# Free matmuls in the pauses of the last stage, its maxima by columns and its blocks half by half, and a third key diagonal in the rotary attention

## The chip, the cores and the metric

One NeuronCore of one Trainium2 chip. The time is the device time of one launch, in microseconds (us). PE is TensorE (PEld its weight loads), DVE VectorE, ACT ScalarE, POOL GpSimd, SP the engine that issues most DMAs.

## The reference, cut to what matters

Two layers over x (16 x 64 tokens of 512 numbers): cross attention over a context, self attention, MLP; each is added to x. The change touches the last two of these six parts.

```
# rotary self attention: 16 heads of 64, 16 sequences of 64 tokens
q, k = rope(xn @ Wq + bq), rope(xn @ Wk + bk);  v = xn @ Wv + bv
x = x + softmax(causal(q @ k.T / 8)) @ v @ Wo + bo
# quantized MLP, I = 1408
fake_quant(t, clip): scale = sigmoid(clip) * max(|t|) / 127
                     return clip(round(t / scale), -128, 127) * scale
xq = fake_quant(layernorm(x), clip_x)                 # max over ALL of x
h  = fake_quant(silu(xq @ wg.T) * (xq @ wu.T), clip_down)  # max over ALL of h
x  = x + h @ wd.T                                     # weights rounded per row
```

Both maxima run over the whole tensor, so nothing can be rounded before the last row of it is there.

## The kernel before

The 1024 tokens are 8 tiles of 128 rows, in `xres`.

**Rotary attention** (`rotary_attention`, L1495) takes two tiles at a time: four turns, the first and the last written out, the two between in a loop. The engines' orders are written by hand, with semaphores. In a turn PE projects four groups of keys and four of queries (n = 0 to 7; group 0 of the keys is done in the turn before), three products of high and low halves each, into `PROJ_BANK`, each group in 24 matmuls. ACT adds the bias (L1743, into `pair`), DVE multiplies by cosine and sine (L1885, two instructions into `s_e`), POOL adds (L1962, L1963) into `kT` or `qT`; `pair` and the products have one buffer, so this chain takes one group after another. The scores of a group (L1624) are one product per pair of heads against a block diagonal of its keys, `k_diag`, that DVE makes from `kT` (`spread_keys`, L1870, two instructions). There are two such buffers for eight groups in a turn (two tiles s, four groups g): group 4s+g waits until the scores of the group two before it are done (L1868). Groups 0 and 1 are spread ahead of the products of n = 4 and 5, all others behind n = 7. Then come the maxima (L1830), exponentials (L1767), transposes, products with the values (`attend`, L1645, which waits for the copies of the values, L1824) and the output projection (L1669), `x` (L1854) and its statistics.

**Last stage** (`FfnFront`, L1395, and `quantized_ffn`, L2294). Each tile is normalised on DVE (L1489), its largest absolute value taken (L1492), transposed on PE (L1461) and copied by ACT (L1466). Tile 7 is last. Then the maximum over columns (L2432), spread over partitions by a transpose (L2369), the step and its inverse (L2438 to L2442). ACT multiplies and rounds `xT` in eight pieces, four per half of the tokens (L2417), DVE clips (L2449, L2451) and makes the steps (L2454). PE multiplies blocks of 128 of the 1408 columns by halves of 512 tokens: gate and up, four matmuls each (L2379 for the first two blocks, L2362 for 20 more), with one pair of banks per half, so a block waits for the multiplication of the block two before it. ACT takes silu (L2423) after gate and up, DVE multiplies (L2459) and takes maxima (L2464), two blocks at a time but one by one for the last two. The second maximum, step and inverse follow; then ACT rounds `inner` tile by tile (L2427; tile 0 in three pieces of 3, 4 and 4 chunks), DVE clips (L2496, L2498), PE multiplies by the down weights, 11 matmuls a tile (L2397), the last tile in two halves (L2405), and DVE scales (L2481). Two of the eight results are added on the core, six by accumulating DMAs of POOL.

Of the kernel before, what the change touches and what calls it, by code (L numbers as in the profile page):

```python
# [17 lines left out]
P = 128  # L18
# [38 lines left out]
class Front:  # L57
# [12 lines left out]
    @staticmethod  # L70
    def reserve(sb, name):

        sb(name, [P, 24 + 2 * D + 4 * KC * P])

# [1196 lines left out]
class RotaryFront:  # L1271


    def __init__(self, core, tag, heads, io, scale):
# [17 lines left out]
        with ExitStack() as early:  # L1292
# [5 lines left out]
            Front.reserve(sb, "over_front")  # L1298
# [96 lines left out]
class FfnFront:  # L1395
# [36 lines left out]
    def open_semaphores(self):  # L1432
# [9 lines left out]
        self.rowmax_ok = sem("rowmax_ok")  # L1442
        self.xT_done = sem("xT_done")
# [9 lines left out]

    def transpose(self, pe, t):
        pe.wait_ge(self.xn_ok, t + 1)
# [37 lines left out]


def rotary_attention(core, block, rot, front, x_done, scale, ffn, finished):  # L1495
# [9 lines left out]
    AHEAD = TURNS  # L1505
    with ExitStack() as st:
# [14 lines left out]
        PROJ_BANK = [6, 7, 0, 1]  # L1521
# [51 lines left out]
        def _(pe):  # L1573
# [34 lines left out]
            def open_scores():  # L1608

                for s in range(2):  # L1610
                    for n in range(NB):
                        pe.matmul(bank[S_BANK[s][n]][:, :], ident_b[:, :], mask_sb[:, :, :].rearrange("p a b -> p (a b)"),
                                  start=True, stop=False, skip_group_check=True)

            def scores(i, s, groups):
                for g in groups:
# [4 lines left out]
                    for a in range(AB):  # L1621
                        for b in range(2):
                            tokens = slice(s * P + b * SEQ, s * P + (b + 1) * SEQ)
                            mm = pe.matmul(at[SEQ * b:SEQ * (b + 1), cols], qT[:, g, a, tokens], k_diag[g % 2][:, a, b, :],  # L1624
                                           start=False, stop=(a == AB - 1), skip_group_check=True)
# [46 lines left out]
            def turn(i, first, last=False):  # L1672
# [50 lines left out]
            for t in range(4, TILES):  # L1723
                ffn.transpose(pe, t)

        @block.scalar
        def _(act):
# [59 lines left out]
            for t in range(2, TILES):  # L1787
                ffn.copy(act, t)

        @block.vector  # L1790
        def _(dve):
# [69 lines left out]
            def turn(i, first, last=False):  # L1861
# [3 lines left out]
                def spread_keys(s, g):  # L1865
                    if 4 * s + g >= 2:

                        dve.wait_ge(s_done, 8 * i + 4 * s + g - 1)  # L1868
                    for a in range(AB):
                        ins = dve.tensor_tensor(  # L1870
                            k_diag[g % 2][:, a, :, :].rearrange("p b (j n) -> p b j n", j=4),
# [4 lines left out]
                for n in range(2 * GROUPS):  # L1876
                    if n in (4, 5):
# [12 lines left out]
                spread_keys(0, 2)  # L1890
# [52 lines left out]
            ffn.normalise(dve, 2, TILES - 1)  # L1943
# [350 lines left out]
def quantized_ffn(core, block, ffn, out):  # L2294
# [6 lines left out]
    HD = D // 2  # L2301
    with ExitStack() as st:
# [20 lines left out]
        g_done = sem("g_done")  # L2323
        silu_ok = sem("silu_ok")
        h_ok = sem("h_ok")
        hmax_ok = sem("hmax_ok")
        hr_a = sem("hr_a")
        hr_b = sem("hr_b")
# [26 lines left out]
        def _(pe):  # L2355
            def gate_and_up(i):
                for s in range(HALVES):
                    if i:
                        pe.wait_ge(h_ok, 2 * (i - 1) + s + 1)
                    for w, bank in ((gT, g_bank), (uT, u_bank)):  # L2360
                        for k in range(KC):
                            mm = pe.matmul(bank[s][:, :], w[:, k, i * P:(i + 1) * P],  # L2362
                                           xT_q[:, k, s * HT:(s + 1) * HT], start=(k == 0), stop=(k == KC - 1))
                    mm.then_inc(g_done, 1)
# [6 lines left out]
            def first_gate_and_up():  # L2371

                pe.wait_ge(gate_in, 16)
                pe.wait_ge(up_in, 16)
                for s in range(HALVES):
                    for k in range(KC):
                        pe.wait_ge(xq_ok, KC * s + k + 1)
                        for w, bank in ((gT, g_bank), (uT, u_bank)):
# [292 lines left out]
```

## Time and profile before

| what | value |
|---|---|
| three runs | 1086.51, 1084.78, 1086.65 us; median 1086.51 |
| profiled execution | 1084.72 us, its span 1082.9 us |
| mean granted clock of PE | 0.995 |
| PE busy | 1053.9 us (97%), x6156 |
| DVE, ACT, POOL busy | 635.0, 347.2, 204.4 us |

A row of a timeline is: start, duration, engine, line, operation, output and inputs, count, and in brackets the idle time of the engine before it and what ended that. Instructions of one line are merged. The granted clock is 1.00 at 2.4 GHz and 0.50 at 1.2 GHz.

### The profile page before, as it was taken

How to read it: one execution, taken by the hardware profiler on the slowest of the kernel's cores; microseconds unless marked ns; L12 is line 12 of the kernel's file. 1: busy time of each engine (PE TensorE's matmuls, PEld its weight loads, DVE VectorE, ACT ScalarE, POOL GpSimd, SP SyncE). 2: the span in 40 equal slices, each digit the busy share in tenths (PEclk: the TensorE clock that was granted, in tenths of full speed). 3: DMA queues.
4: the chain of work that ended last, by engine and by line, in shares of the span. 5: the costliest groups of instructions: out<-in, count | busy, mean ns of one | idle time of the engine just before them, and what ended most of it. 6: DMA issues, size and time to landing. Idle time of an engine off the chain costs nothing.

```text
span 1082.9 us, 16786 instructions
## 1 busy us (share of the span) xinstructions
PE 1053.9 (97%) x6156; PEld 660.2 (61%) x6172; DVE 635.0 (59%) x1116; ACT 347.2 (32%) x984; POOL 204.4 (19%) x201
## 2 busy tenths in 40 slices
PE   9999999999999999999999999999999999999887
PEld 5556658888544444444444466657788696877333
DVE  3344346877856621357652275557866758468677
ACT  2422256566521110220001032236332524226434
POOL 0011101333222230000002511131214133040002
PEclk9999999999999999999999999999999999999998
DMA  9996802001026680025547469963000000040105
GB/s 349 378 335 220 331 1 79 2 0 40 20 95 205 118 38 1 0 84 165 168 120 266 159 210 365 367 238 117 2 1 1 2 1 0 0 156 16 59 1 77
DMA packets 68609, 129.59 MB, mean 120 GB/s; under 512 B 9424, under 2 KB 13520, under 8 KB 68176
## 3 DMA queue, kind: packets, MB, share of 16 engines
q1 hardware_dynamic: 67696, 127.38, 36.3%
q0 software_dynamic: 864, 1.57, 1.2%
q8 instruction: 29, 0.48, 0.2%
q14 instruction: 20, 0.16, 0.0%
HBM read 120.92 MB, written 8.01 MB: 119 GB/s over the span
## 4 chain that ended last, share of the span: by engine, by line
PE 66%; issue 11%; DVE 10%; POOL 5%; ACT 3%; SPq 2%; DMA 1%; DVEq 0%; POOLq 0%; ACTq 0%
PE bank L2126 26%; PE bank L2153 5%; PE bank L474 5%; PE bank L442 4%; PE bank L396 3%; PE bank L2362 3%; PE bank L972 2%; PE bank L1669 2%; PE bank L519 2%; PE bank L508 2%; DVE s_e L1885 2%; PE bank L2397 2%; ACT s_e L1063 2%; PE bank L494 2%; DMA x_proj<-in_x_pw_dram 1%
## 5 line engine op out<-in xcount | busy, mean ns | idle before, releaser
L2171 ACT ACTIVATE f_act<-bank,f_sgn 128x512 f32<-128x512 f32 x64 | 44.0, 687 | 261.8 <-PE bank L2126 257.3
L2126 PE MATMUL bank<-f_a_lo,f_w 128*128 128x512 f16 x512 | 115.7, 379 | 0.0
L2126 PE MATMUL bank<-f_a_hi,f_w 128*128 128x512 f16 x512 | 115.7, 379 | 0.0
L2126 PEld LDWEIGHTS bank<-f_a_lo,f_w 128*128 x512 | 50.1, 98 | 60.4
L2126 PEld LDWEIGHTS bank<-f_a_hi,f_w 128*128 x512 | 50.1, 98 | 60.2
L2226 DVE CAST f_b_hi<-f_act 128x512 f16<-128x512 f32 x32 | 26.6, 833 | 96.9 <-ACT f_act L2171 96.8
L1885 DVE TENSOR_TENSOR s_e<-s_pair,s_tables 128x512 f32<-128x512 f32 x64 | 41.4, 688 | 37.2 <-POOL s_kT L1963 21.6
L442 PE MATMUL bank<-x_cT,x_qT 128*64 128x512 f32 x256 | 58.5, 598 | 0.0
L474 PE MATMUL bank<-x_cN,x_eT 128*64 128x512 f32 x256 | 56.9, 596 | 0.0
L1767 ACT ACTIVATE s_e<-bank,s_nmax 128x64 f32<-128x64 f32 x128 | 38.1, 337 | 31.5 <-DVE s_nmax L1830 31.3
L2282 POOL TENSOR_SCALAR f_w<-f_upper_bits 128x2048 bf16<-128x2048 uint8 x16 | 31.3, 1957 | 76.1 <-PE bank L2126 76.1
L1870 DVE TENSOR_TENSOR s_k_diag<-s_kT,s_spread 128x512 f32<-128x512 f32 x64 | 44.6, 754 | 1.1 <-PE bank L1624 1.0
L738 DVE TENSOR_TENSOR x_aT_lo<-bank,x_aT_hi 128x512 fp32r<-128x512 f32 x16 | 11.1, 691 | 56.6 <-ACT x_aT_hi L599 56.5
L1063 ACT ACTIVATE s_e<-bank,s_nmax 128x64 f32<-128x64 f32 x128 | 38.1, 350 | 7.0 <-DVE s_nmax L1134 6.9
L773 POOL TENSOR_TENSOR x_mv<-x_mv,eps 128x2 f32<-128x2 f32 x10 | 1.9, 192 | 200.5 <-DVE x_mv L631 200.5
L474 PEld LDWEIGHTS bank<-x_cN,x_eT 128*64 128x64 f32 x256 | 17.6, 137 | 32.8 <-issue 32.6
L1624 PE MATMUL bank<-s_k_diag,s_qT 128*64 128x256 f32 x256 | 32.9, 389 | 3.6 <-DVE s_k_diag L1870 2.1
L442 PEld LDWEIGHTS bank<-x_cT,x_qT 128*64 128x64 f32 x256 | 16.9, 136 | 31.2 <-issue 30.8
L1962 POOL TENSOR_TENSOR s_kT<-s_e 128x256 f32<-128x256 f32 x16 | 13.3, 832 | 111.7 <-DVE s_e L1885 111.7
L780 POOL MEMSET x_ones<- 128x128 f32 x1 | 0.2, 204 | 179.3 <-DMA x_bk<-in_x_kb_dram 179.3
L2262 DVE SCALAR_TENSOR_TENSOR xres<-bank,f_out_scale,xres 128x512 f32<-128x512 f32 x8 | 6.0, 751 | 47.0 <-PE bank L2153 47.0
L2126 PE MATMUL bank<-f_xT_hi,f_w 128*128 128x512 f16 x128 | 32.9, 379 | 0.0
(341 smaller groups left out, 2309.4 us busy)
## 6 DMA issues: line engine op xcount, KB each, us to landing
x_cT<-in_ctx_cols_dram SPq DMA_DIRECT2D x32, 1024.0 KB, 9.0
x_cN<-in_ctx_rows_dram SPq DMA_DIRECT2D x32, 1024.0 KB, 11.6
f_upper_bits<-in_f_w_dram SPq DMA_DIRECT2D x20, 256.0 KB, 4.1
f_row<-in_f_wg_dram SPq DMA_DIRECT2D x11, 256.0 KB, 3.2
f_long_row<-in_f_wd_dram SPq DMA_DIRECT2D x4, 704.0 KB, 6.4
f_row<-in_f_wu_dram SPq DMA_DIRECT2D x11, 256.0 KB, 3.1
f_part<-in_f_wgT_dram SPq DMA_DIRECT2D x8, 352.0 KB, 3.5
f_part<-in_f_wuT_dram SPq DMA_DIRECT2D x8, 352.0 KB, 3.2
```

The source lines that it names most:

```text
L396: mm = pe.matmul(bank[Q_BANK[half]][:, a * PT:(a + 1) * PT], l[:, k, c * P:(c + 1) * P], r[:, k, :], start=(m == 0 and k == 0), stop=(m == ...
L442: mm = pe.matmul(bank[S_BANK[s]][SEQ * b:SEQ * (b + 1), :], qT[:, k, tokens], cT[s][:, b, k, :], start=(k == 0), stop=(k == KC - 1))
L474: mm = pe.matmul(bank[AV_BANK[s]][SEQ * b:SEQ * (b + 1), :], eT[s][:, k, SEQ * b:SEQ * (b + 1)], cN[s][:, b, k, :], start=(k == 0), stop=( ...
L1063: ins = act.activation(e_sb[s][n][:, j * SEQ:(j + 1) * SEQ], bank[S_BANK[s][n]][:, j * SEQ:(j + 1) * SEQ], ACT.Exp, bias=nmax[s][:, h:h + ...
L1624: mm = pe.matmul(at[SEQ * b:SEQ * (b + 1), cols], qT[:, g, a, tokens], k_diag[g % 2][:, a, b, :], start=False, stop=(a == AB - 1), skip_gr ...
L1767: ins = act.activation(e_sb[n][:, j * SEQ:(j + 1) * SEQ], bank[S_BANK[s][n]][:, j * SEQ:(j + 1) * SEQ], ACT.Exp, bias=nmax[s][:, h:h + 1], ...
L1870: ins = dve.tensor_tensor(k_diag[g % 2][:, a, :, :].rearrange("p b (j n) -> p b j n", j=4), kT[:, g, a, s * P:(s + 1) * P].rearrange("p (b ...
L1885: ins = dve.tensor_tensor(flat(prods[t]), flat(pair[:, :, :]), table(t), ALU.mult)
L2126: mm = pe.matmul(h_bank[s][:, :], weights(2 * i + s, k), part[:, k, cols], start=(n == 0 and k == 0), stop=(n == 1 and k == k_chunks - 1))
L2153: mm = pe.matmul(y_bank[t % 2][:, :], part[:, k, t * P:(t + 1) * P], w2_sb[:, k, :], start=(n == 0 and k == 0), stop=(n == 1 and k == HC - 1))
L2171: act.activation(act32[s][:, :], h_bank[s][:, :], ACT.Relu, scale=sgn[:, layer % 2:layer % 2 + 1]).then_inc(h_read, 1)
L2362: mm = pe.matmul(bank[s][:, :], w[:, k, i * P:(i + 1) * P], xT_q[:, k, s * HT:(s + 1) * HT], start=(k == 0), stop=(k == KC - 1))
```

## The change

In the last stage of `rotary_attention` and in `quantized_ffn`:

- `keep_busy` issues matmuls whose result nobody reads: 8 behind the transposes of tiles 4 to 6, 6 behind that of tile 7, 7 behind the last block and 9 behind the second spread of the maxima.
- Tile 7 is centred first (no root needed), its maximum taken and that column multiplied by the root; ACT scales the rows beside it. The spread of the maxima now stands ahead of tile 7's transposes, and ACT rounds the first half of `xT` before it copies tile 7.
- The first four blocks go (0,0), (1,0), (0,1), (1,1) (column block, half); banks and silu buffers go by block number. Gate and up have a semaphore each, so silu starts after the gate.
- DVE multiplies and rounds the first piece of `inner` itself; ACT starts with the second.

In the rotary attention a third `k_diag` lies in the place of the normalised rows; keys of group 2 are spread ahead of n = 6; groups 2 and 3 are projected into banks 2 and 3; the masks of the first tile and its first scores no longer wait for the last read of the queries.

```diff
+        slots.append(sb("k_diag2", shape))
+    def keep_busy(self, pe, count, free):
+        for _ in range(count):
+            pe.matmul(self.core.bank[free][:, :], self.gT[:, 0, 0:P], self.gT[:, 0, 0:D], start=True, stop=True)
+    def centre_last(self, dve):
+        t = TILES - 1
+        dve.wait_ge(self.xT_done, t - 5)
+        dve.tensor_scalar(self.xn[t % 6][:, :], self.core.xres[:, t, :], self.mv[:, t, 0:1], None, ALU.subtract).then_inc(self.centred, 1)
+        dve.wait_ge(self.centred, 1)
+        dve.tensor_reduce(self.a_rows[:, t:t + 1], self.xn[t % 6][:, :], AX_X, ALU.max, apply_absolute_value=True).then_inc(self.centred, 1)
+        dve.wait_ge(self.centred, 2)
+        dve.wait_ge(self.rstd_ok, 3)
+        dve.tensor_tensor(self.a_rows[:, t:t + 1], self.a_rows[:, t:t + 1], self.rstd[:, t:t + 1], ALU.mult).then_inc(self.rowmax_ok, 1)
+    def scale_last(self, act):
+        act.wait_ge(self.centred, 2)
+        act.wait_ge(self.rstd_ok, 3)
+        act.activation(self.xn[t % 6][:, :], self.xn[t % 6][:, :], ACT.Copy, scale=self.rstd[:, t:t + 1]).then_inc(self.last_ok, 1)
...
-        PROJ_BANK = [6, 7, 0, 1]
+        PROJ_BANK = [6, 7, 2, 3]
-                    if n == 2:
-                        pe.wait_ge(x_ok, 2 * i + 1)
...
                 pe.wait_ge(k_read, GROUPS * (i + 1))
+                pe.wait_ge(x_ok, 2 * i + 1)
+                open_scores(0)
+                scores(i, 0, (0, 1))
                 pe.wait_ge(q_read, GROUPS * (i + 1))
-                open_scores()
-                scores(i, 0, (0, 1))
+                open_scores(1)
                 project_values(0, (1,))
...
-            for t in range(4, TILES):
+            for t in range(4, TILES - 1):
                 ffn.transpose(pe, t)
+            pe.wait_ge(ffn.gate_in, 16)
+            ffn.keep_busy(pe, 8, 5)
...
-                    if 4 * s + g >= 2:
-                        dve.wait_ge(s_done, 8 * i + 4 * s + g - 1)
+                    n = 4 * s + g
+                    if n >= KD:
+                        dve.wait_ge(s_done, 8 * i + n - KD + 1)
-                    if n in (4, 5):
+                    if n in (4, 5, 6):
                         spread_keys(0, n - 4)
                 copy_values(i, 0, (0,))
-                spread_keys(0, 2)
                 spread_keys(0, 3)
...
+    BLOCKS = [(0, 0), (1, 0), (0, 1), (1, 1)] + [(i, s) for i in range(2, IC) for s in range(HALVES)]
...
             spread_maxima(0)
-            first_gate_and_up()
-            for i in range(1, IC):
-                gate_and_up(i)
+            ffn.transpose(pe, TILES - 1)
+            pe.wait_ge(up_in, 16)
+            ffn.keep_busy(pe, 6, 5)
+            for n in range(len(BLOCKS)):
+                if n in (0, 2):
+                    gate_and_up_by_chunk(n)
+                else:
+                    gate_and_up(n)
+            pe.wait_ge(h_ok, len(BLOCKS) - 1)
+            ffn.keep_busy(pe, 7, 4)
             spread_maxima(1)
+            ffn.keep_busy(pe, 9, 4)
...
-            act.wait_ge(xT_ok, TILES)
+            act.wait_ge(xT_ok, TILES // 2)
             for s in range(HALVES):
+                if s == 1:
+                    ffn.copy(act, TILES - 1)
+                    act.wait_ge(xT_ok, TILES)
...
+                if n == 0:
+                    dve.tensor_scalar(part, part, a_inv[:, 1:2], ROUND, ALU.mult, ALU.add).then_inc(first_ok, 1)
+                    dve.wait_ge(first_ok, 1)
+                else:
+                    dve.wait_ge(hr_a, n)
```

## Rows read from the trace of the kernel before

**Rows 1.** The page: its span, and PE's granted clock in 40 slices (tenths)

```profile
span 1082.9 us, 16786 instructions
...
PEclk9999999999999999999999999999999999999998
```

**Rows 2.** Timeline of DVE in the third turn of the rotary attention

```profile
890.17 1.29 DVE L1885 TENSOR_TENSOR s_e<-s_pair,s_tables 128x512 f32<-128x512 f32 x2 [0.63 <-POOL s_kT L1963]
891.38 1.84 DVE L1870 TENSOR_TENSOR s_k_diag<-s_kT,s_spread 128x512 f32<-128x512 f32 x2
893.84 1.29 DVE L1885 TENSOR_TENSOR s_e<-s_pair,s_tables 128x512 f32<-128x512 f32 x2 [0.63 <-POOL s_qT L1963]
896.68 1.29 DVE L1885 TENSOR_TENSOR s_e<-s_pair,s_tables 128x512 f32<-128x512 f32 x2 [1.54 <-POOL s_qT L1963]
...
904.99 0.69 DVE L1830 TENSOR_REDUCE s_nmax<-bank 128x8 f32<-128x512 f32 x1
905.96 2.50 DVE L1870 TENSOR_TENSOR s_k_diag<-s_kT,s_spread 128x512 f32<-128x512 f32 x4 [0.28 <-PE bank L1624]
```

**Rows 3.** Timeline of POOL in the same turn

```profile
891.54 1.13 POOL L1962 TENSOR_TENSOR s_qT<-s_e 128x256 f32<-128x256 f32 x1 [1.41 <-DVE s_e L1885]
892.62 1.19 POOL L1963 TENSOR_TENSOR s_qT<-s_e 128x256 f32<-128x256 f32 x1
895.22 0.73 POOL L1962 TENSOR_TENSOR s_qT<-s_e 128x256 f32<-128x256 f32 x1 [1.41 <-DVE s_e L1885]
```

**Rows 4.** Timeline of PE in the same turn: the products with the values

```profile
913.21 1.97 PE L1645 MATMUL bank<-s_v_diag,s_pT 128*64 128x128 f32 x32
```

**Rows 5.** Timeline of DVE in the first turn and in the last

```profile
774.41 0.69 DVE L1830 TENSOR_REDUCE s_nmax<-bank 128x8 f32<-128x512 f32 x1
775.59 2.50 DVE L1870 TENSOR_TENSOR s_k_diag<-s_kT,s_spread 128x512 f32<-128x512 f32 x4 [0.49 <-PE bank L1624]
...
971.10 0.69 DVE L1830 TENSOR_REDUCE s_nmax<-bank 128x8 f32<-128x512 f32 x1
971.71 2.50 DVE L1870 TENSOR_TENSOR s_k_diag<-s_kT,s_spread 128x512 f32<-128x512 f32 x4
```

**Rows 6.** Timeline of all engines from tile 7 to the last block

```profile
1007.42 0.55 DVE L1489 TENSOR_SCALAR f_xn<-xres,f_mv,f_rstd 128x512 f32<-128x512 f32 x1 [0.67 <-POOL f_rstd L1482]
1008.71 0.59 ACT L1466 COPY f_xT<-bank 128x512 f32<-128x512 f32 x1 [1.79 <-PE bank L1461]
1010.14 5.75 ACT L2417 ACTIVATE f_xT<-f_xT,f_plus_round,f_a_inv 128x512 f32<-128x512 f32 x8 [0.84 <-DVE f_a_inv L2442]
1016.70 0.74 DVE L2459 SCALAR_TENSOR_TENSOR f_inner<-bank,f_step,f_silu 128x512 f32<-128x512 f32 x1
1017.50 1.04 PE L2362 MATMUL bank<-f_xT_q,f_gT 128*128 128x512 bf16 x4
...
1050.86 1.03 PE L2362 MATMUL bank<-f_xT_q,f_gT 128*128 128x512 bf16 x4
```

**Rows 7.** PE by quarter microseconds: length, busy time (count), granted clock, DMA share, GB/s

```profile
1056.25:1056.50 0.25, 0.00 (x0) 0.72 0.00 0
...
1063.00:1063.25 0.25, 0.25 (x2) 0.63 0.00 0
```

**Rows 8.** Timeline of all engines from the last silu to the second tile's product

```profile
1052.79 0.69 ACT L2423 ACTIVATE f_silu<-bank,f_step 128x512 f32<-128x512 f32 x1 [1.04 <-PE bank L2362]
1055.02 0.18 DVE L2476 TENSOR_REDUCE f_a_max<-f_h_max 128x1 f32<-128x22 f32 x1
1058.14 0.58 PE L2397 MATMUL bank<-f_dT,f_inner_q 128*128 128x512 bf16 x1 [2.57 <-DVE f_inner_q L2498]
1061.00 0.56 DVE L2498 TENSOR_SCALAR f_inner_q<-f_inner_q 128x1408 bf16<-128x1408 bf16 x1
1062.79 1.44 PE L2397 MATMUL bank<-f_dT,f_inner_q 128*128 128x512 bf16 x5
```

**Rows 9.** Groups of ACT by shape: ACT's first piece of `inner`

```profile
L2427 ACT ACTIVATE f_inner<-f_inner,f_plus_round,f_a_inv 128x384 f32<-128x384 f32 x1 | 0.7, 707 | 2.9 <-DVE f_a_inv L2442 2.9
```

More of the change, by code:

```diff
@@ L1505, in rotary_attention @@
     AHEAD = TURNS
+    KD = len(rot.k_diag)
     with ExitStack() as st:
@@ L1606, in project_values, with open_scores @@
                     mm.then_inc(v_done, 1)
[L1608 to L1613, printed above, removed]
+            def open_scores(s):
+                for n in range(NB):
+                    pe.matmul(bank[S_BANK[s][n]][:, :], ident_b[:, :], mask_sb[:, :, :].rearrange("p a b -> p (a b)"),
+                              start=True, stop=False, skip_group_check=True)
             def scores(i, s, groups):
@@ L1786, in _ @@
             act.preload_act_table(ACT.Silu)
-            for t in range(2, TILES):
+            for t in range(2, TILES - 1):
                 ffn.copy(act, t)
+            ffn.scale_last(act)
         @block.vector
@@ L2355, in _, with gate_and_up, gate_and_up_by_chunk @@
         def _(pe):
[L2356 to L2364, printed above, removed]
+            def gate_and_up(n):
+                i, s = BLOCKS[n]
+                if n >= 2:
+                    pe.wait_ge(h_ok, n - 1)
+                for w, bank, done in ((gT, g_bank, g_done), (uT, u_bank, u_done)):
+                    for k in range(KC):
+                        mm = pe.matmul(bank[n % 2][:, :], w[:, k, i * P:(i + 1) * P],
+                                       xT_q[:, k, s * HT:(s + 1) * HT], start=(k == 0), stop=(k == KC - 1))
+                    mm.then_inc(done, 1)
+            def gate_and_up_by_chunk(n):
+                i, s = BLOCKS[n]
+                if n >= 2:
+                    pe.wait_ge(h_ok, n - 1)
+                for k in range(KC):
+                    pe.wait_ge(xq_ok, KC * s + k + 1)
+                    for w, bank, done in ((gT, g_bank, g_done), (uT, u_bank, u_done)):
+                        mm = pe.matmul(bank[n % 2][:, :], w[:, k, i * P:(i + 1) * P], xT_q[:, k, s * HT:(s + 1) * HT],
+                                       start=(k == 0), stop=(k == KC - 1))
+                        if k == KC - 1:
+                            mm.then_inc(done, 1)
             def spread_maxima(n):
@@ L2418, in _ @@
             act.wait_ge(steps_ok, 2)
-            for i in range(IC):
-                for s in range(HALVES):
-                    act.wait_ge(g_done, 2 * i + s + 1)
-                    act.activation(silu[s][:, :], g_bank[s][:, :], ACT.Silu, scale=steps[0][:, i:i + 1]).then_inc(silu_ok, 1)
+            for n, (i, s) in enumerate(BLOCKS):
+                act.wait_ge(g_done, n + 1)
+                if n >= 2:
+                    act.wait_ge(h_ok, n - 1)
+                act.activation(silu[n % 2][:, :], g_bank[n % 2][:, :], ACT.Silu, scale=steps[0][:, i:i + 1]).then_inc(silu_ok, 1)
             act.wait_ge(astep_ok, 4)
-            for t, chunks in PIECES:
+            for t, chunks in PIECES[1:]:
                 part = inner[:, chunks, t * P:(t + 1) * P]
```

63 lines of the change are left out of this document (34 added, 29 removed).

## The prediction

> **What bounds the kernel now.** The page first: PE is granted its full clock in every slice but the last [rows 1], so the change has to be read from the timelines of two stretches, the rotary attention (four turns) and the last stage. In the rotary attention the timeline of DVE is what ends last between the last rope of a turn and the products with the values: DVE runs copy, spreads, maxima and spreads with one short wait, and PE's products with the values start when DVE's copies are there [rows 2, 4]. In the last stage four things follow each other that PE can't shorten: the maximum of x, the rounding of x, the maximum of h, the rounding of h. Rows 6 and 8 are that chain. Its last part is run at half clock: the granted clock leaves 1.00 inside 1056.25:1056.50, after a stretch in which PE had done one transpose since 1052.8, and is back inside 1063.00:1063.25 [rows 7]. It fell once before, about 1012, inside the first chain.
>
> **Rotary attention.** A rope group comes every 2.84 us (893.84 to 896.68), and every 3.67 us where a spread stands ahead of it (890.17 to 893.84): 0.83 us more, because POOL's two additions take 1.13 and 1.19 us beside the spread and 0.73 alone [rows 2, 3]. A third spread at n = 6 thus delays the last rope of a turn by 0.83 us. In return one spread of four halves, half of 2.50, so 1.25 us, goes from DVE's run behind the last rope [rows 2]. And the spread of the second tile's group 0 waits for a diagonal: from maximum to spread it takes 0.97 us in the third turn (904.99 to 905.96), 1.18 in the first (774.41 to 775.59), and 0.61 in the last, where nothing is waited for [rows 2, 5]. With three diagonals it needs the scores of the group three before it, which PE has then done. So a turn gains 1.25 - 0.83 = 0.42, plus 0.57, 0.36, 0.36 and 0 us of that wait: 0.99 + 0.78 + 0.78 + 0.42 = 2.97 us. I take 2.9. What is late next is PE itself: it would finish its second transposes some 0.3 us ahead of the copies, so up to 0.8 us a turn fits, barely. PE's own earlier masks and scores are worth nothing on top, since DVE decides when `attend` starts; they cover that the last read of the queries also comes 0.83 us later. The wait that is added (x_ok ahead of the first masks) has project_outputs and add of the turn before behind it, some 20 us ago. The banks only change who waits, at nothing: the banks 2 and 3 were read long before. Bounds: the spread's cost is between nothing (POOL's time alone) and 1.25 us (all of it), the gain of a turn between 0 (another engine takes over at once) and 1.25 + 0.57; for four turns 0 to 5 us, and if the delay came back nowhere, a loss of 4 x 0.83 = 3.3.
>
> The Trainium skill bears on the third spread. Its page "SBUF — State Buffer", section "Who interferes with whom", says that a VectorE instruction with two SBUF inputs contends with a GpSimd one that reads SBUF, and that the second to issue is blocked until the first has ended. Taken strictly, one addition would wait for most of one spread half and the next for all of another, about 1.2 us a turn for 0.83, and the four turns would gain 1.5 us for 2.9. The rows have 0.83, so I keep that.
>
> **The first chain.** Centring doesn't wait for the root: the 0.67 us in which DVE waited for POOL go [rows 6]; one multiplication of a column is added, about 0.2 us (the column reduction at 1055.02 takes 0.18 [rows 8]). The inverse is there 0.45 us earlier. But ACT's eight pieces (5.75 us, 0.71 apart) now have the copy of tile 7 in their middle, 0.59 us alone, some 0.62 with its wait [rows 6]; before, that copy lay in ACT's idle time. ACT's last piece ends 0.15 us later than before, and DVE multiplies only after it has clipped all eight pieces. So the first multiplication stays at about 1016.75 and the third block of PE at 1017.55 against 1017.50 [rows 6]: +0.05 us. Blocks (0,0) and (1,0) are both done by about 1015.6 and PE stands idle for 2 us; nothing comes of the new order. Bounds: if the copy were free, -0.45; if the scaling on ACT (a piece of 0.8 us, finished about when the inverse is there) pushed the pieces back by all of it, +0.8.
> The free matmuls here cost nothing: at 0.22 us each (four in 1.04 with the last one's own time [rows 6]) the 8 end at about 1007.8, ahead of the spread at 1008.5, and the 6 at about 1011.0, ahead of the first clipped piece at 1011.4. That half clock near 1012 slowed only matmuls that waited for DVE anyway.
>
> **The blocks.** From the third block (1017.50) to the last (1050.86) are 19 blocks in 33.36 us, 1.756 each; eight matmuls at 0.216 make 1.73 [rows 6]. The difference is the wait for the multiplication of two blocks before. With silu behind the gate alone it ends 0.87 us earlier, so the wait is met: -0.5 us. The same at the end: the last product ends at 1052.76, silu, multiplication and maximum follow, and the reduction starts at 1055.02, 2.26 us later [rows 8]. With silu already done, the multiplication starts at once, and DVE is free by then; 0.69 + 0.03 us of silu go: -0.7 us. Bounds: 0, where DVE is the one that is late, to -0.87.
>
> **The second chain and the down product.** The first product starts at 1058.14 and has its 11 matmuls in 4.65 us (0.42 each, the half clock), so the second tile starts at 1062.79 [rows 8]. Its input had been ready since 1061.56 (1061.00 + 0.56). At full clock tile 0 takes 2.4 us and the second tile would start at 1061.6; the two matmuls at half clock behind 1062.79 cost 0.3 more: the clock is worth 1.5 us. With ACT's first piece (0.707 us, 0.62 to the next [rows 9]) done by DVE instead, ACT reaches tile 1 0.62 us earlier, and the second tile, which waits for that and not for PE, starts 0.62 us earlier again. That the first product starts 0.4 us earlier is worth nothing. After that PE runs 2.375 us a tile as now. Together -2.1 us. Does the clock hold? Between the last block and the down product PE would have 7 free matmuls (1.5 us), 0.4 us idle, a transpose, 9 more (1.9 us) and 0.3 us idle, against one transpose in 5.4 us. The 9 end before the first product could start. Bounds for this part: 0 (the clock falls all the same and ACT's piece is lost in it) to -2.6.
>
> **The sum** for the profiled execution: -2.9 + 0.05 - 0.5 - 0.7 - 2.1 = -6.2 us (rounded), 1084.72 to 1078.5. That execution was as fast as the fastest of the three runs (1084.78), 1.8 us under their median of 1086.51. From the median the same sum gives 1080.3. Part of the spread can be the clock's fall, which the change takes away; I can't tell how much, and put the median in the middle, at 1079.4.
>
> **The rivals.**
> Clock lost in the second pause. A free matmul may not count, or not enough: the clock falls at about 1056 as now and stays low for 6.8 us [rows 7]. Then the 9 free matmuls take 3.8 us for 1.9 and hold the first product back by 1.65, and tile 0 runs slow: second tile 2.7 us later than planned, 1078.5 + 2.7 = 1081.2, by the median 1082.1. For it: transposes around 1009 didn't prevent the fall. Against it: real matmuls of this shape brought the clock back both times.
> Rotary gain not there. The rope chain is 0.83 us late, and what DVE saves is taken by PE or ACT (exponentials, transposes) as the next bound: 0 instead of -2.9, 1082.3 by the median. For it: PE would be only 0.3 us ahead.
> On the other side: the rope chain becomes what ends last in each turn. If something else than DVE's run held `attend` back, the 0.83 us would be paid in all four turns (+3.3 instead of -2.9) and the result is 1079.4 + 6.2 = 1085.6, level; it is slower only if in addition to being late each spread costs POOL its full 1.25: +5.0 instead of -2.9, 1087.3. It decides from a delay of 0.83 + 0.2 us per turn with no return. Against it: the last turn shows DVE's run without any wait, from the last rope to the copies.
> The change doesn't do what it says: the free matmuls are there and the clock is full, but DVE, at 0.95 + 0.56 + 0.75 us a tile against 2.375, sets the down product's pace after the early start: 1.5 us of the 2.1 lost, 1080.9.
>
> **How the numbers follow.** Forecast 0.62, with its own range 1077.5 to 1081; clock lost 0.14; rotary gain missing 0.12; DVE's pace 0.07; the other side 0.05. The range reaches to the first two rivals and leaves out the other side: 1077.2 to 1083.0. A measurement of this kernel can tell 0.2%, 2.2 us, from no change. Faster by more: 0.93; within: 0.04 (the other side's level half and mishaps of two rivals at once); slower: 0.03.
>
> **What would show it.** The trace after: rope groups 3.67 us apart three times a turn; no wait of DVE for L1624's banks; `attend` 0.4 to 1 us earlier relative to the turn's start, turns of 64.5 us for 65.3. In the last stage: ACT's copy of tile 7 between its fourth and fifth piece, the third block 0.0 to 0.2 us from where it was relative to tile 7's statistics, blocks 1.73 us apart, 1.5 us from the last product to the second reduction, clock at 1.00 from there to the end, and the second tile's product waiting about 0.85 us for DVE with PE idle. The prediction is wrong if the clock is 0.50 anywhere behind 1050, if the turns stay at 65.3 us, or if the third block comes over 0.5 us earlier or later.

## The result, and the profile after

| | before | after |
|---|---|---|
| median | 1086.58 us (1084.78 to 1088.05, 4 runs) | 1079.36 us (1078.92 to 1079.75, 4 runs) |
| profiled execution | 1084.72 us, span 1082.9 | 1079.72 us, span 1077.8 |
| mean granted clock | 0.995 | 1.000 |

The ratio is 0.9937, 95% interval [0.9924, 0.9951]: faster by 0.6%, 6.8 us by the ratio. The forecast was 1079.4. The page after, span and granted clock by slices [rows 1]:

```profile
span 1077.8 us, 16886 instructions
...
PEclk9999999999999999999999999999999999999999
```

Cut at events that both kernels have, the two traces give the table (us; "sum of row t" is the start of DVE's addition of tile t to x; the block times are PE's). The first sum of x stands ahead of the four turns.

| stretch | before | after | difference | predicted |
|---|---|---|---|---|
| start to the sum ahead of the turns (nothing changed) | 745.85 | 747.00 | +1.15 | 0 |
| the four turns, to the sum of row 7 | 259.07 | 255.89 | -3.18 | -2.9 |
| to the third block | 12.58 | 12.47 | -0.11 | +0.05 |
| 19 blocks, to the start of the last | 33.36 | 32.82 | -0.54 | -0.5 |
| to the second reduction | 4.16 | 3.44 | -0.72 | -0.7 |
| to the second inverse | 1.19 | 1.18 | -0.01 | 0 |
| to the halves of the last tile | 21.02 | 19.07 | -1.95 | -2.1 |
| to the end of the span | 5.67 | 5.93 | +0.26 | 0 |
| outside the span | 1.82 | 1.92 | +0.10 | 0 |

The changed stretches give -6.51, the others +1.51, together the -5.00 between the two profiled executions. The +1.15 is not the change's: over the fourteen kernels profiled here, with the same work up to that point, the sum starts between 745.65 and 747.00, and this execution is the highest. Nor is the +0.26: that last stretch takes 5.64 to 6.22 us in the others.

**The rotary attention.** DVE in the third turn after, and the first two of PE's products with the values; the rows answer to [rows 2, 4]:

```profile
889.63 1.29 DVE L1924 TENSOR_TENSOR s_e<-s_pair,s_tables 128x512 f32<-128x512 f32 x2 [0.63 <-POOL s_kT L2001]
...
893.30 1.29 DVE L1924 TENSOR_TENSOR s_e<-s_pair,s_tables 128x512 f32<-128x512 f32 x2 [0.63 <-POOL s_qT L2001]
894.51 1.83 DVE L1909 TENSOR_TENSOR s_k_diag<-s_kT,s_spread 128x512 f32<-128x512 f32 x2
896.97 1.29 DVE L1924 TENSOR_TENSOR s_e<-s_pair,s_tables 128x512 f32<-128x512 f32 x2 [0.63 <-POOL s_qT L2001]
899.79 1.29 DVE L1924 TENSOR_TENSOR s_e<-s_pair,s_tables 128x512 f32<-128x512 f32 x2 [1.52 <-POOL s_qT L2001]
...
902.74 1.29 DVE L1909 TENSOR_TENSOR s_k_diag<-s_kT,s_spread 128x512 f32<-128x512 f32 x2
904.06 0.69 DVE L1868 TENSOR_REDUCE s_nmax<-bank 128x8 f32<-128x512 f32 x1
904.67 2.49 DVE L1909 TENSOR_TENSOR s_k_diag<-s_kT,s_spread 128x512 f32<-128x512 f32 x4
...
910.08 1.73 DVE L1862 TENSOR_TENSOR s_v_diag<-bank,s_bv_row 64x256 f32<-64x256 f32 x4
911.90 0.33 PE L1677 MATMUL bank<-s_v_diag,s_pT 128*64 128x128 f32 x2
```

A group with a spread ahead of it comes 3.67 us behind the one before (893.30 to 896.97), one without 2.82. Behind the last rope two spread halves are left for four, and the four behind the first maximum start 0.61 us after it and run without a wait, for 0.97 before [rows 2]. The products with the values start 36.25 us into the turn (from the sum of row 3, at 875.65) for 37.03 before (from 876.18) [rows 4]. The turns take 64.10, 64.55, 64.52 and 62.72 us, before 65.05, 65.28, 65.29 and 63.45: gains of 0.95, 0.73, 0.77 and 0.73.

**The first pause.** All engines after, which answers to [rows 6]:

```profile
1007.23 0.17 DVE L2496 RECIPROCAL f_a_inv<-f_a_step 128x1 f32<-128x1 f32 x1
1007.48 2.93 ACT L2471 ACTIVATE f_xT<-f_xT,f_plus_round,f_a_inv 128x512 f32<-128x512 f32 x4 [0.89 <-DVE f_a_inv L2496]
1010.31 0.56 ACT L1484 COPY f_xT<-bank 128x512 f32<-128x512 f32 x1
1010.91 2.93 ACT L2471 ACTIVATE f_xT<-f_xT,f_plus_round,f_a_inv 128x512 f32<-128x512 f32 x4
1014.56 1.41 DVE L2515 SCALAR_TENSOR_TENSOR f_inner<-bank,f_step,f_silu 128x512 f32<-128x512 f32 x2
1015.36 0.39 PE L2415 MATMUL bank<-f_xT_q,f_gT 128*128 128x512 bf16 x1 [1.78 <-DVE f_inner L2515]
```

ACT's copy of tile 7 stands between its fourth and fifth piece, and PE idles 1.78 us ahead of the third block.

**The second pause**, after, which answers to [rows 8]; L1467 are the free matmuls:

```profile
1049.24 0.69 ACT L2477 ACTIVATE f_silu<-bank,f_step 128x512 f32<-128x512 f32 x1 [1.04 <-DVE f_inner L2515]
...
1050.11 0.75 DVE L2515 SCALAR_TENSOR_TENSOR f_inner<-bank,f_step,f_silu 128x512 f32<-128x512 f32 x1
1050.89 0.69 DVE L2521 TENSOR_REDUCE f_h_max<-f_inner 128x1 f32<-128x512 f32 x1
1051.62 0.17 DVE L2533 TENSOR_REDUCE f_a_max<-f_h_max 128x1 f32<-128x22 f32 x1
...
1052.01 2.11 PE L1467 MATMUL bank<-f_gT 128*128 128x512 bf16 x9
...
1052.80 0.16 DVE L2496 RECIPROCAL f_a_inv<-f_a_step 128x1 f32<-128x1 f32 x1
...
1054.42 2.54 PE L2448 MATMUL bank<-f_dT,f_inner_q 128*128 128x512 bf16 x11 [0.30 <-DVE f_inner_q L2559]
...
1056.01 0.96 DVE L2557 TENSOR_SCALAR f_inner_q<-f_inner 128x1408 bf16<-128x1408 f32 x1 [0.42 <-ACT f_inner L2481]
...
1057.61 4.71 PE L2448 MATMUL bank<-f_dT,f_inner_q 128*128 128x512 bf16 x21 [0.66 <-DVE f_inner_q L2559]
```

Silu of the last block runs beside its second product. Tile 0 of the down product takes 2.54 us to the end of its last matmul; before it was 4.65 from its start to that of tile 1 [rows 8]. Then PE stands idle until DVE has clipped tile 1, and DVE had itself waited 0.42 for ACT.

### The profile page after: what moved, and what is told of

It reads as the page before. It is cut to its first block, busy times and chain, and to the rows that moved or that the text cites. A ratio compares the mean times of both kernels' runs of the same rounds, so it can differ in the third digit from the quotient of the medians.

```text
span 1077.8 us, 16886 instructions
## 1 busy us (share of the span) xinstructions
PE 1056.4 (98%) x6186; PEld 663.5 (62%) x6202; DVE 638.7 (59%) x1118; ACT 347.2 (32%) x984; POOL 207.9 (19%) x201
## 4 chain that ended last, share of the span: by engine, by line
PE 65%; issue 11%; DVE 10%; POOL 6%; ACT 3%; SPq 3%; DMA 1%; DVEq 0%; POOLq 0%; ACTq 0%
PE bank L2164 26%; PE bank L2191 5%; PE bank L482 5%; PE bank L450 4%; PE bank L404 3%; PE bank L2403 3%; PE bank L980 2%; PE bank L1701 2%; PE bank L527 2%; PE bank L516 2%; DVE s_e L1924 2%; ACT s_e L1071 2%; PE bank L502 2%; DMA x_proj<-in_x_pw_dram 1%; PE bank L2448 1%
## 5 line engine op out<-in xcount | busy, mean ns | idle before, releaser
L1909 DVE TENSOR_TENSOR s_k_diag<-s_kT,s_spread 128x512 f32<-128x512 f32 x64 | 47.1, 787 | 0.1
```

What stands on the lines that cost most here:

```text
L1909: ins = dve.tensor_tensor(k_diag[n % KD][:, a, :, :].rearrange("p b (j n) -> p b j n", j=4), kT[:, g, a, s * P:(s + 1) * P].rearrange("p ( ...
```

## The experiments

The twelve kernels were measured in three groups, each beside the kernel before, whose median moved between them (1085.81, 1085.37, 1085.94). So medians are compared within a group only, and across groups the ratios and the stretches of the traces, by the cuts of the table above.

### The rotary part alone

```
# the kernel before, with only the edits in rotary_attention and k_diag2
```

> The kernel before with the rotary edits alone; the last stage is untouched. Theory (DVE's run behind the last rope ends last in a turn, and a third diagonal shortens it): the four turns are 0.95, 0.73, 0.77 and 0.73 us shorter, as in the trace after, 3.2 us in all, and the time is 3.2 us under that of before. The last stage keeps both stretches at half clock, so the spread between runs stays as wide as that of before. Rival (the rotary edits move nothing of their own; the turns are shorter because of something in the last stage's code): turns of 65.3 us as before, no gain.

1082.60 us against 1085.81, ratio 0.9970 [0.9958, 0.9981], 3.2 us. Its four turns take 255.85 us, as in the changed kernel (255.89), 3.22 less than before. The rotary part adds up with the rest, and no engine outside DVE took the gain back. The clock still falls: 0.51 in 1053 to 1060. The seven runs lie within 1.3 us, the eleven of the kernel before beside them within 3.0, so the spread did not stay as wide as expected. The last stage is that of before, yet the stretch from the second inverse to the halves takes 20.80 us for 21.02: where the clock comes back moves it by 0.22 us between executions.

### No free matmuls, and those of the first pause alone left out

```diff
-        for _ in range(count):
+        for _ in range(0):
```

> The changed kernel without all 30 free matmuls; nothing else differs. Theory (only the second pause matters, because the first blocks wait for DVE): granted clock 0.50 again near the first blocks and from the second maximum into the down product. The down product's second tile starts 1.5 to 2 us later than in the changed kernel, the end comes 1.5 us later (0 to 3.4 us, by where the clock's fall and rise lie), and the third block starts where it did. Rival (the clock would hold anyway with the shorter pauses): clock 1.00, no difference. Rival (the first pause matters too): the third block or the blocks behind it are late, over 3 us in all.

```diff
-            ffn.keep_busy(pe, 8, 5)
...
-            ffn.keep_busy(pe, 6, 5)
```

> The changed kernel without the 8 and 6 free matmuls of the first two pauses; the 7 and 9 of the last two stay. Theory: the clock falls near the first blocks only, where PE waits for DVE, and costs 0 to 0.5 us; the down product starts and runs as in the changed kernel. Rival (a fall there is not over when the third block starts): the blocks behind 1015 run at half clock for up to 3 us, 1.5 us lost.

Without any: 1080.57 us (ratio 0.9953 [0.9939, 0.9967]); without the first 14: 1079.11 (0.9936 [0.9923, 0.9950]). Busy times by stretch without any free matmul (columns: length; PE, PEld, DVE, ACT, POOL busy with counts; granted clock; DMA share; GB/s):

```profile
1051.00:1053.00 2.00, 0.29 (x1) 0.13 (x1) 1.36 (x5) 0.78 (x2) 0.00 (x0) 0.63 0.00 0
1053.00:1058.00 5.00, 4.35 (x11) 1.64 (x12) 4.42 (x10) 5.00 (x5) 0.00 (x0) 0.50 0.00 0
```

and PE there, from the second block's last product to the third block:

```profile
1013.38 1.31 PE L2403 MATMUL bank<-f_xT_q,f_uT 128*128 128x512 bf16 x4
1014.54 0.38 PE L2415 MATMUL bank<-f_xT_q,f_gT 128*128 128x512 bf16 x1
```

Without those of the first pause:

```profile
1008.00:1010.00 2.00, 1.42 (x4) 0.66 (x6) 1.90 (x7) 1.97 (x4) 0.00 (x0) 0.50 0.98 369
1010.00:1013.00 3.00, 3.00 (x9) 1.04 (x8) 2.61 (x10) 3.00 (x5) 0.00 (x0) 0.50 0.75 279
...
1051.00:1053.00 2.00, 2.00 (x10) 0.70 (x8) 1.64 (x6) 1.09 (x2) 0.00 (x0) 1.00 0.00 0
```

From the inverse to the halves it is 20.53 us without any, and 19.08 with those of the second pause, as in the changed kernel (19.07): the clock is worth 1.46 us there. In the first pause the clock is 0.50 for 6.8 us in both kernels, and without the first 14 alone that costs nothing: from the sum of row 7 to the second reduction 48.73 us with them and 48.73 without, since PE waits there for DVE either way. Without any it takes 48.88. By the granted clock in half microseconds it came back some 0.8 us later behind the sum of row 7 in that execution (12.1 us for 11.2); PE had no idle time left ahead of the third block, as the rows show, and that block starts 12.64 us behind the sum for 12.47. So DVE hides the half clock with next to no margin: 0.00 us lost in one execution, 0.15 in the other. The stretch from the second reduction to the inverse is 0.07 longer without any as well (1.25 for 1.18); no cause of that is shown. All 30 free matmuls together are worth 1.68 us by these stretches.

### A third pair of banks

```diff
+    BLOCKS = [(0, 0), (1, 0), (2, 0), (0, 1), (1, 1), (2, 1)] + [(i, s) for i in range(3, IC) for s in range(HALVES)]
+    SETS = 3
-        core.bank[2:4], core.bank[4:6], core.bank[6:8]
+        core.bank[2:4], core.bank[4:6] + [core.bank[1]], core.bank[6:8] + [core.bank[2]]
-                if n >= 2:
-                    pe.wait_ge(h_ok, n - 1)
+                if n >= SETS:
+                    pe.wait_ge(h_ok, n - SETS + 1)
# the chunk-wise blocks are 0 and 3; free matmuls behind the last block go into bank 5
```

> The changed kernel with a third pair of banks (1 and 2, free by then) for gate and up: the first six blocks go (0,0), (1,0), (2,0), (0,1), (1,1), (2,1), a block waits for the multiplication of the block three before it, and the free matmuls of the last pauses go to bank 5. Theory (PE is idle for 1.8 us ahead of the third block only because both pairs of banks are taken, and DVE, with 1.33 us of work a block against PE's 1.73, catches up before the last block): the third block runs in that pause and all behind it come one block earlier, 1.7 us gained on the changed kernel. Rival (DVE's first multiplication at 1014.6 is the true start of the pipeline and its backlog reaches the end): 0 to 0.5 us gained.

1076.72 us (1076.32 to 1077.94), ratio 0.9918 [0.9904, 0.9931], 2.4 us under the kernel without the first free matmuls in the same group, of which 1.73 is the edit's by the traces; 0.57 lies in the last stretch (5.65 us for 6.22), which no edit touches. The stretch to the second reduction takes 47.00 us for 48.73, a whole block of 1.73 less. PE's idle time ahead of the third block is filled with one more block of the first half, and PE gets to the fourth (the first that needs the second half) only 0.2 us before DVE's multiplication frees its banks:

```profile
1013.26 1.41 DVE L2516 SCALAR_TENSOR_TENSOR f_inner<-bank,f_step,f_silu 128x512 f32<-128x512 f32 x2
1014.07 0.39 PE L2416 MATMUL bank<-f_xT_q,f_gT 128*128 128x512 bf16 x1
```

### ACT's first piece of h given back

```diff
-            for t, chunks in PIECES[1:]:
+            for t, chunks in PIECES:
...
-                if n == 0:
-                    dve.tensor_scalar(part, part, a_inv[:, 1:2], ROUND, ALU.mult, ALU.add).then_inc(first_ok, 1)
```

> The changed kernel, but ACT rounds the first piece of `inner` again and DVE only clips it. Theory: the second tile of the down product waits for ACT's fourth piece, so it starts one ACT piece (0.62 us from start to start) later and PE ends that much later; everything ahead of the second inverse as in the changed kernel: from the inverse to the last tile's halves 19.7 us for 19.07, time 1079.4 + 0.6 = 1080.0. Rival: DVE's clipping sets the pace of that stretch and not ACT: 0, 1079.4, and the wait ahead of the second tile as long as in the changed kernel.

1079.22 us, ratio 0.9944 [0.9931, 0.9958]. The time alone doesn't tell it from the changed kernel, the trace does: from the inverse to the halves 19.67 us for 19.07, +0.60. DVE waits for ACT ahead of tile 1, and PE behind it:

```profile
1055.44 0.96 DVE L2553 TENSOR_SCALAR f_inner_q<-f_inner 128x1408 bf16<-128x1408 f32 x1 [0.69 <-ACT f_inner L2481]
...
1057.05 5.14 PE L2448 MATMUL bank<-f_dT,f_inner_q 128*128 128x512 bf16 x23 [0.94 <-DVE f_inner_q L2555]
```

### Silu behind both products, with two waits and with one

```diff
-                act.wait_ge(g_done, n + 1)
+                act.wait_ge(u_done, n + 1)
```

> The changed kernel, but ACT's silu waits for the end of `up` and not of `gate`. Theory: the blocks are 1.756 us apart again for 1.727 (19 of them: +0.5 us) and the last product is followed by silu, multiplication and maximum in a row again (2.26 us to the second reduction for 1.55: +0.7), together +1.2, time 1080.6, and from the sum of row 7 to the second reduction 49.95 us for 48.73. Rival: the blocks were 1.727 apart because of the order of the blocks and silu buffers, not of the silu's start: only +0.7, 1080.1.

1080.50 us, ratio 0.9956 [0.9942, 0.9969]. From the sum of row 7 to the second reduction it takes 50.77 us, +2.04 and not +1.2. The blocks are 1.794 us apart, more than before the change (1.756). DVE here waits for the product and then for silu, and starts 0.10 us behind silu's end; before it was one wait and 0.03. So that was taken away:

```diff
-                dve.wait_ge(u_done, n + 1)
                 dve.wait_ge(silu_ok, n + 1)
```

> As the run with silu behind both products, but DVE's multiplication waits for silu alone and not for the product and silu. That run had the blocks 1.794 us apart and a multiplication 0.10 us behind silu's end, the kernel before 1.756 and 0.03. Theory: the second wait costs 0.07 us and stands in the loop that sets the pace there, so without it the blocks are 1.756 apart again, 0.7 us less in all: from the sum of row 7 to the second reduction 50.0 us for 50.77. Rival: the order of blocks or the silu buffers set it, and it stays at 50.7.

1079.75 us, ratio 0.9948 [0.9934, 0.9961]; 49.97 us to the second reduction, the blocks 1.756 apart. The last block with two waits:

```profile
1049.97 0.69 ACT L2477 ACTIVATE f_silu<-bank,f_step 128x512 f32<-128x512 f32 x1 [1.04 <-PE bank L2403]
1050.76 0.75 DVE L2515 SCALAR_TENSOR_TENSOR f_inner<-bank,f_step,f_silu 128x512 f32<-128x512 f32 x1 [0.25 <-ACT f_silu L2477]
```

and with one:

```profile
1049.52 0.69 ACT L2477 ACTIVATE f_silu<-bank,f_step 128x512 f32<-128x512 f32 x1 [1.04 <-PE bank L2403]
1050.24 0.75 DVE L2514 SCALAR_TENSOR_TENSOR f_inner<-bank,f_step,f_silu 128x512 f32<-128x512 f32 x1 [0.17 <-ACT f_silu L2477]
```

From the start of silu to that of the multiplication it is 0.79 us against 0.72. The early silu is worth 49.97 - 48.73 = 1.24 us, as the two terms of the prediction say. The second wait that the change adds costs 0.07 us a multiplication where it lies on the path (why an already satisfied wait costs that, no run shows), so 0.04 a block (1.794 for 1.756), since a block waits for the multiplication of the block two before, and 0.8 in all; in the changed kernel a multiplication ends some 0.7 us before its banks are needed, which hides it.

### Tile 7 as before, and tile 7 rounded straight from its bank

```diff
-            act.wait_ge(xT_ok, TILES // 2)
+            act.wait_ge(xT_ok, TILES)
...
-            ffn.centre_last(dve)
+            ffn.normalise(dve, 2, TILES - 1)
# transposes of tile 7 ahead of the spread, its copy ahead of ACT's rounding
```

> The changed kernel, but tile 7 is normalised, its maximum taken, transposed and copied ahead of the spread and of ACT's rounding, as before the change; the free matmuls, the order of the blocks and the semaphores stay. Theory: the inverse is 0.45 us later and ACT's last rounding piece at most 0.15 us from where it was, so the third block starts within 0.15 us of where it does (12.47 us behind the sum of row 7; 12.58 in the kernel before): time 1079.3 to 1079.5. Rival: the new order is worth what it takes from the inverse's path: +0.45, third block 12.9 us behind, 1079.85.

1079.02 us, ratio 0.9942 [0.9928, 0.9955]; the third block is 12.58 us behind the sum of row 7 for 12.47. The whole new order of tile 7 is worth 0.1 us. ACT's pieces start 0.63 us later relative to the sum of row 7 (5.22 us behind it for 4.59), but run without the copy in their middle and end level (10.97 us behind it for 10.95):

```profile
1007.52 5.75 ACT L2464 ACTIVATE f_xT<-f_xT,f_plus_round,f_a_inv 128x512 f32<-128x512 f32 x8 [0.84 <-DVE f_a_inv L2489]
...
1014.08 1.40 DVE L2508 SCALAR_TENSOR_TENSOR f_inner<-bank,f_step,f_silu 128x512 f32<-128x512 f32 x2
1014.88 0.39 PE L2412 MATMUL bank<-f_xT_q,f_gT 128*128 128x512 bf16 x1 [1.25 <-DVE f_inner L2508]
```

```diff
-                    ffn.copy(act, TILES - 1)
+                    act.activation(xT[:, :, (TILES - 1) * P:], ffn.bank[TILES - 1][:, :].rearrange("p (k n) -> p k n", k=KC),
+                                   ACT.Identity, bias=plus_round[:, 0:1], scale=a_inv[:, 0:1]).then_inc(xr_a, 1)
# and the four pieces of the second half only 384 wide
```

> The changed kernel, but ACT no longer copies tile 7: it multiplies and rounds it straight out of its bank in one instruction (128x512), and its four pieces of the second half shrink to 384 columns. Theory: from the inverse to the third block ACT is what ends last, so four pieces shorter by about 0.1 us each (0.62 from start to start for 0.72, as the 128x384 and 128x512 pieces of the second rounding show) bring the third block 0.4 us forward, from 12.47 to 12.07 us behind the sum of row 7: 1079.0. Rival: DVE's clipping (0.67 to 0.72 us a piece) is as late as ACT and takes the place: at most 0.1, 1079.3.

1079.44 us (1078.25 to 1081.00), ratio 0.9944 [0.9930, 0.9957]: the times tell nothing of 0.2 us. By the trace the third block is 12.28 us behind the sum of row 7, -0.2, half of what ACT saves (its last piece ends 10.58 us behind the sum for 10.95):

```profile
1010.10 2.49 ACT L2473 ACTIVATE f_xT<-f_xT,f_plus_round,f_a_inv 128x384 f32<-128x384 f32 x4
...
1010.82 0.43 DVE L2505 TENSOR_SCALAR f_xT_q<-f_xT 128x512 bf16<-128x512 f32 x1 [0.23 <-ACT f_xT L2473]
...
1011.49 0.42 DVE L2505 TENSOR_SCALAR f_xT_q<-f_xT 128x512 bf16<-128x512 f32 x1
```

DVE waits for the first of these pieces only and then clips one in 0.67 us without a pause: it has taken ACT's place. Neither theory is right by itself: in the changed kernel ACT ends last, but only 0.2 us behind what DVE's own pace would allow.

### Two diagonals, and the masks back in their place

```diff
-                    if n in (4, 5, 6):
+                    if n in (4, 5):
...
+                spread_keys(0, 2)
                 spread_keys(0, 3)
# and k_diag2 gone, so KD = 2
```

> The changed kernel with two key diagonals for three (keys of group 2 spread behind the last rope again), the banks of groups 2 and 3 and the place of the masks and first scores as changed. Theory: all of the rotary gain is DVE's, so it goes: from the sum of x that ends turn 0 to that of turn 3 as in the kernel before, some 0.75 us a turn longer, 3.2 us for four turns: 1082.6. Rival: PE's masks and scores ahead of the last read of the queries carry a part of it, in the wait for the diagonals (0.97, 0.97, 0.61 us from maximum to spread before): then turns of 64.9 and 1.2 to 1.6 us in all, 1080.6 to 1081.

1081.65 us, ratio 0.9963 [0.9950, 0.9977]. The turns take 258.61 us: 2.72 of the 3.18 us went, and 0.46 stay with PE's order, less than the rival said and more than the theory. The masks' place was then turned back with three diagonals:

```diff
                 pe.wait_ge(x_ok, 2 * i + 1)
-                open_scores(0)
-                scores(i, 0, (0, 1))
                 pe.wait_ge(q_read, GROUPS * (i + 1))
+                open_scores(0)
                 open_scores(1)
+                scores(i, 0, (0, 1))
```

> The changed kernel with three diagonals, but PE's masks and first scores wait for the last read of the queries again. The run with two diagonals lost 2.72 us over the turns of the 3.18 gained, so 0.46 is left for PE's order. Theory A: that 0.46 is a part of the wait for a diagonal, which three diagonals take away anyway: here nothing is lost, the turns from the sum of row 1 to that of row 7 take 255.9 us. Theory B: it is a gain of its own and adds up: 256.35 us.

1081.01 us, ratio 0.9955 [0.9941, 0.9968]; the turns take 257.26 us, 1.37 more than 255.89, about 0.34 in each. Both theories fall: nothing lost, and 256.35. DVE's third turn shows what ends last then:

```profile
903.87 0.69 DVE L1868 TENSOR_REDUCE s_nmax<-bank 128x8 f32<-128x512 f32 x1
904.48 1.28 DVE L1909 TENSOR_TENSOR s_k_diag<-s_kT,s_spread 128x512 f32<-128x512 f32 x2
906.05 1.29 DVE L1909 TENSOR_TENSOR s_k_diag<-s_kT,s_spread 128x512 f32<-128x512 f32 x2 [0.30 <-PE bank L1656]
```

The spread of the second tile's group 0 starts at once, as the third diagonal lets it; that of its group 1 needs the scores of group 2 and waits 0.30 us for them, as in the other three turns (0.28 to 0.29). The four corners, in us for the four turns:

| | masks late | masks early |
|---|---|---|
| two diagonals | 259.07 | 258.61 |
| three diagonals | 257.26 | 255.89 |

Alone the edits are worth 1.81 and 0.46, together 3.18: 0.91 us come only with both. The corner with two diagonals and masks late is the kernel before, which also has groups 2 and 3 in banks 0 and 1 and the wait for `x_ok` there; no run has these alone, so their share of 1.81 and 0.46 is not shown.

### Three pairs of banks with tile 7 rounded from its bank, and tile 1 of h cut in two

```diff
+    SECOND = (0, 6, IC)
-                    pe.wait_ge(hq_ok, len(FIRST) - 1 + t)
+                    pe.wait_ge(hq_ok, len(FIRST) + t)
+                    if t == 1 and k in SECOND:
+                        pe.wait_ge(hq_ok, len(FIRST) + SECOND.index(k))
```

> The kernel with three pairs of banks, with two more edits: ACT rounds tile 7 straight out of its bank, and the rounding and clipping of tile 1 of h is cut in two (6 and 5 column blocks), so that the down product of tile 1 can start with the first six. Theory: PE idled 0.2 us ahead of the fourth block and 0.75 us between tile 0 and tile 1 of the down product; both go, from the sum of row 7 to the second reduction 46.8 us for 47.00 and from the inverse to the last tile's halves 18.3 us for 19.07: ratio to the kernel before 0.9909 for 0.9918. Rival: the cut costs DVE an instruction pair more and DVE is late with tile 2 instead: only 0.3 us of the 0.95, 0.9915.

1077.47 us (1076.70 to 1077.69), ratio 0.9921 [0.9907, 0.9934]: as fast as with the third pair of banks alone. The first part came (46.80 us to the second reduction for 47.00); the second didn't: 19.15 us from the inverse to the halves for 19.07. Tile 1 now follows tile 0 with no idle time, and tile 2 waits instead:

```profile
1051.71 4.91 PE L2452 MATMUL bank<-f_dT,f_inner_q 128*128 128x512 bf16 x22 [0.31 <-DVE f_inner_q L2565]
...
1055.02 0.96 DVE L2563 TENSOR_SCALAR f_inner_q<-f_inner 128x1408 bf16<-128x1408 f32 x1 [0.42 <-ACT f_inner L2487]
...
1056.49 0.73 DVE L2544 SCALAR_TENSOR_TENSOR f_xT<-bank,f_a_step,f_d_row 128x512 f32<-128x512 f32 x1
...
1057.37 12.03 PE L2452 MATMUL bank<-f_dT,f_inner_q 128*128 128x512 bf16 x55 [0.75 <-DVE f_xT L2544]
```

Tile 2 goes into tile 0's bank, which DVE reads only after it has clipped tile 2, and for that it waits 0.42 us for ACT. Cutting tile 1 moved the wait by one tile. The best version that was run is the one with three pairs of banks; this one is not told apart from it.

## Why the prediction was right, point by point

**Rotary attention**: -2.9 predicted, -3.18 by the trace, -3.22 in the rotary part alone. The delay of a spread was read rightly (3.67 for 2.84 us), and the three first turns came within 0.05 us of 0.99, 0.78 and 0.78. The last gained 0.73 for 0.42: the last rope there came only 0.48 us later relative to the turn's start (965.62 from 941.47 before, 964.80 from 940.17 after), since a gap of 0.35 us ahead of it in the kernel before is gone. The bound of 0.8 us a turn, taken from PE's lead, didn't hold either: the first turn gained 0.95. The bounds of the four turns were added up wrongly, too: by the prediction's own terms, 1.25 us a turn and the waits, the upper one is 6.3 us and not 5. The strict reading of the Trainium skill, "SBUF — State Buffer", section "Who interferes with whom", under which I gave the turns 1.5 us, is not borne out: the trace has 0.85 us a spread after the change (3.67 for 2.82), for 0.83 before.

The step "PE's own earlier masks and scores are worth nothing on top" fails. The sum gave the wait for a diagonal wholly to the third diagonal, "which PE has then done"; with the masks late PE has not done it for group 1, and a new wait of 0.34 us stands in each turn. That the sum came out is luck here: the change had both edits. I had looked for a new wait at the end of the turn, 0.3 us of lead of PE, and not at the second spread of the run.

**The first chain**: +0.05 predicted, -0.11. The inverse comes 0.63 us earlier for 0.45, and that this would be eaten is borne out by tile 7 in its old order (+0.11). That it is ACT alone that eats it is only half right: with ACT 0.4 us shorter DVE's clipping takes over after 0.2. The free matmuls of the first pause are worth nothing, as predicted, but with no margin: without any free matmul the third block was 0.17 us late.

**The blocks and the last product**: -0.5 and -0.7 predicted, -0.54 and -0.72. What I left out is the price of the wait that the change adds for DVE, u_done: 0.07 us a multiplication, 0.8 in all. It is hidden in this kernel and would have cost more than the -0.5 if silu had stayed behind both products.

**The down product**: -2.1 predicted, -1.95. The parts measure 1.46 for the clock (predicted 1.5) and 0.60 for ACT's piece (0.62). That the first product's earlier start is worth nothing is seen where ACT has that piece back: the first product comes 0.32 us later behind the inverse (1.94 for 1.62), and the whole loss is ACT's 0.60. The two parts exceed the whole by 0.11 because each was measured with the other in place. From the kernel before, the clock alone is worth 21.02 - 19.67 = 1.35 us and ACT's piece alone, at half clock, 21.02 - 20.53 = 0.49; in either order it is 1.95. That at half clock the piece is worth only the 0.31 us by which the first product starts earlier, since PE and not ACT is then what tile 1 waits for, would explain the difference, but is not shown: this stretch moved by 0.22 us between two executions of the same last stage (21.02 and 20.80). PE waited 0.66 us ahead of tile 1, for the 0.85 foretold.

**The rivals.** The clock stayed at 1.00 from the last block on. DVE doesn't set the pace of the down product: PE waits for it once, then the tiles are 2.375 us apart and DVE's work takes 2.1. Nothing but DVE's run was seen to hold `attend` back: in the third turn the products with the values start 0.09 us behind DVE's copies (911.90 for 911.81), 0.78 us earlier in the turn than before. Two of the rivals' times, 1082.1 and 1082.3, are called "by the median", but are counted from 1079.4; from the median's 1080.3 they are 1083.0 and 1083.2, so the range up to 1083.0 just misses the second.

**The level.** From the profiled execution the sum gave 1078.5; it was 1079.72, since the unchanged part was 1.15 us later in this execution. From the median it gave 1080.3; the measured 6.8 us by the ratio, with 5.3 to 8.3 in its interval, hold the 6.5 that the stretches show. The forecast of 1079.4 was a middle chosen between the two, and that the median came to 1079.36 is luck. That the fall of the clock widens the spread of the runs can't be read here: the clock falls in the kernel without any free matmul and in the one with the rotary edits alone, and their runs lie within 1.4 and 1.3 us.

## What to carry to other kernels

A pause of PE in front of its own work is worth filling with matmuls that nobody reads only where PE, once it starts, is what ends last: here 1.46 us in one pause, and 0.00 and 0.15 in two executions without them in the other. Look instead for real work that could fill the pause: one block more in a third pair of banks was worth 1.73 us, as much as all free matmuls together (1.68). Where a buffer is added, follow every later reader of the ring and not only the one that waits today: the gain of the third diagonal was 1.81 us alone and 2.72 with PE's scores moved ahead.

## What the runs showed of the hardware

- Two semaphore waits in front of a DVE instruction, the first of them satisfied some 0.7 us before the second, cost 0.07 us more than the second alone: 0.79 us from silu's start to the multiplication for 0.72, and 1.794 us a block for 1.756.
- POOL's root of one column took 0.72 us beside DVE's centring of 128x512, and 0.56 us beside nothing of DVE's; in the eleven kernels here that centre tile 7 it took 0.72 or 0.73, in the three that don't 0.55 or 0.56. The row before the change:

```profile
1006.83 0.56 POOL L1482 TENSOR_TENSOR f_rstd<-f_var,minus_half 128x1 f32<-128x1 f32 x1 [6.68 <-DVE f_var L1478]
```

and after:

```profile
1004.63 0.48 DVE L1516 TENSOR_SCALAR f_xn<-xres,f_mv 128x512 f32<-128x512 f32 x1
...
1004.80 0.72 POOL L1500 TENSOR_TENSOR f_rstd<-f_var,minus_half 128x1 f32<-128x1 f32 x1 [6.69 <-DVE f_var L1496]
```

- Work that no edit touched moved by 1.35 us between profiled executions (745.65 to 747.00 for the same point). Edits of under 1 us could be told only by stretches cut at events near them. Where the clock falls inside a stretch, even that moved by 0.22 us (21.02 and 20.80 for the same last stage).
